# Gate and up projections of a quantised FFN from bare 4-bit values, with the PSUM bank rescaled between scale groups

## What is computed

```python
vals = _FP4_LUT[nib].reshape(out_f, in_p * 8)      # 0, 0.5, 1 ... 6 and their negatives
w = vals * repeat(scales.T, 128, axis=1)           # gate_up: [2*1408, 512], 4 groups of inputs
gate_up = x @ w_gu.T;  h = silu(gate) * up         # I = 1408
y = h @ w_down.T;  y / sqrt(mean(y * y) + 1e-6)    # down: 11 groups of inputs
```

## Time and profile before

| | us |
|---|---|
| median of 3 runs | 812.85 (810.42 to 815.97) |
| the profiled execution | 812.29 |
| its span, first to last instruction | 810.5 |
| PE busy in the span | 716.4 (88%) |
| DVE busy | 498.3 (61%) |
| ACT busy | 386.4 (48%) |
| POOL busy | 195.8 (24%) |

### The profile page before, as it was taken

The page is one execution under the profiler, slowest core; times in us unless marked ns, Lnnn a source line. Parts: engine busy times, 40 slices in busy tenths (PEclk is TensorE's granted clock), DMA queues, the critical chain, the costliest instruction groups (busy, mean ns, idle before and its releaser), DMA issues.

```text
span 810.5 us, 11696 instructions
## 1 busy us (share of the span) xinstructions
PE 716.4 (88%) x4565; PEld 571.0 (70%) x4574; DVE 498.3 (61%) x956; ACT 386.4 (48%) x617; POOL 195.8 (24%) x229
## 2 busy tenths in 40 slices
PE   5899999999999996689998898898988898899993
PEld 4688777887777785467676666676667676678883
DVE  4658668765587667667456567665577575643424
ACT  4345453447444633743635363646463745452324
POOL 0554344454453559411210000211000211000000
PEclk9999999999999998679999999999999999999997
DMA  9500101003200310120001130030120030000201
GB/s 324 181 16 10 44 2 40 15 1 118 66 14 2 118 54 1 66 90 1 1 27 52 53 104 0 1 130 0 53 105 0 1 130 0 20 34 1 104 1 53
DMA packets 25408, 41.17 MB, mean 51 GB/s; under 512 B 5002, under 2 KB 7690, under 8 KB 25226
## 3 DMA queue, kind: packets, MB, share of 16 engines
q1 hardware_dynamic: 23194, 37.40, 13.4%
q10 hardware_dynamic: 2160, 3.02, 1.1%
HBM read 28.88 MB, written 11.53 MB: 50 GB/s over the span
## 4 chain that ended last, share of the span: by engine, by line
PE 57%; DVE 22%; ACT 14%; issue 3%; POOL 1%; DMA 1%; ACTq 1%; SPq 0%; DVEq 0%; POOLq 0%
PE ps L1716 14%; PE ps L1730 11%; PE ps L1304 10%; PE ps L1388 3%; PE ps L1693 3%; PE ps L529 2%; PE ps L1694 2%; PE ps L1343 2%; PE ps L538 2%; DVE small L417 2%; ACT w L280 2%; DVE act_s L378 2%; DVE w L410 2%; DVE masked L1223 2%; DVE act_s L410 1%
## 5 line engine op out<-in xcount | busy, mean ns | idle before, releaser
L1716 PE MATMUL ps<-x2T_hi,weights 128*128 128x512 f32 x528 | 164.1, 392 | 0.0
L1716 PEld LDWEIGHTS ps<-x2T_hi,weights 128*128 128x128 f32 x528 | 99.9, 189 | 20.4
L1730 PE MATMUL ps<-weights,h_hi 128*128 128x512 f32 x352 | 110.8, 397 | 0.7 <-DVE h_lo L1578 0.6
L1716 PE MATMUL ps<-x2T_lo,weights 128*128 128x512 f32 x264 | 108.6, 411 | 0.4
L1601 DVE TENSOR_TENSOR silu<-ps,silu 128x512 f32<-128x512 f32 x44 | 30.4, 690 | 124.0 <-PE ps L1716 106.3
L1304 PE MATMUL ps<-wqkv_lo,xT_hi 128*128 128x512 f32 x192 | 81.3, 424 | 9.7 <-DVE wqkv_lo L1172 5.7
L1730 PEld LDWEIGHTS ps<-weights,h_hi 128*128 128x128 f32 x352 | 66.9, 191 | 16.0 <-DVE h_lo L1578 1.8
L1304 PE MATMUL ps<-wqkv_hi,xT_hi 128*128 128x512 f32 x192 | 76.6, 399 | 0.0
L1304 PE MATMUL ps<-wqkv_hi,xT_lo 128*128 128x512 f32 x192 | 76.4, 398 | 0.0
L1100 POOL TENSOR_TENSOR rot<-qkv,tab 128x256 f32<-128x256 f32 x64 | 44.8, 733 | 116.1 <-ACT qkv L989 116.1
L1730 PE MATMUL ps<-weights,h_lo 128*128 128x512 f32 x176 | 69.4, 394 | 0.0
(11 more groups left out here) (190 smaller groups left out, 1518.9 us busy)
## 6 DMA issues: line engine op xcount, KB each, us to landing
w<-in_fside_BxS2xS_dram SPq DMA_DIRECT2D x4, 1024.0 KB, 5.3
x_dram<-xb SPq DMA_DIRECT2D x4, 1024.0 KB, 4.3
xc<-x_dram SPq DMA_DIRECT2D x4, 1024.0 KB, 5.6
x_in<-in_x_dram SPq DMA_DIRECT2D x15, 256.0 KB, 3.5
xb<-x_dram SPq DMA_DIRECT2D x3, 1024.0 KB, 5.6
out_dram<-xc SPq DMA_DIRECT2D x3, 1024.0 KB, 4.3
z<-in_x_dram SPq DMA_DIRECT2D x3, 768.0 KB, 5.0
x_dram<-z SPq DMA_DIRECT2D x3, 768.0 KB, 3.5
```

Of the source, the lines that this page charges most:

```text
L1716: last = nc.tensor.matmul(dst[:, :], lhs, rhs, start=False, stop=(k == NK - 1 and n == 2), skip_group_check=True)
L1730: last = nc.tensor.matmul(ps[c][:, :], lhs, rhs, start=(it == 0 and n == 0), stop=(it == NI - 1 and n == 2))
```

## The change

Gate and up keep bare values in all four groups. A group is two matmuls (values by `x2T_lo`, values by `x2T_hi`) per half, and after groups 0, 1 and 2 the bank is multiplied in place by the ratio of this group's scale to the next one's; the last scale goes into the silu's `scale` and into the product with up. Gate is now rescaled by ACT (`scale_gate`), up by DVE (`scale_up`), three times each per tile. The ratios are made once on DVE (`column_ratios`, after chunk 1; a zero scale becomes 2^-80).

What comes with it:

- A tile is cut into four rounds. A round is group k of gate, group k of up and one chunk (three matmuls) of a down product; there are now 44 places per batch, one behind each round (place n is behind round n mod 4 of tile n div 4).
- All 24 gate and up pieces are bare. ACT copies the ones of even number, DVE those of odd number; only the 11 down pieces still take a diagonal, `hi` and `lo`. 18 pieces are made in chunks 14 and 15 and behind them, 17 beside the first batch (`PIECE_SLOTS`). The last layer norm of attention (`LATE_STEPS`) moves into the first batch as well.
- The output of down is copied out of its banks at the start of the next batch (`copy_y`, DVE, four times), and the residual and final scaling of the output (before on DVE) are done by POOL. So are the column scaling of the expert's weights (through a copy of the row on ACT, `w_rows_out`, `v_rows_out`) and the sum behind the expert (`add01`, `add23`).
- `EXPERT_STEPS`, `EXPERT0_STEPS` and `OUTPUT_STEPS` have new places; two maxima of the batch after next are taken at places 40 and 43.

```diff
+EXPERT_STEPS = {"w_maxima": 0, "w_maxima2": 4, "x_maxima": 2, "columns": 6, "x_maxima2": 5, "ratio": 6, "root": 7,
+                "smooth": 7, "rows": 8, "scale_x": 8, "max_x": 8, "round_x": 10, "clip_x": 11, "w_rows_out": 10,
+                "pool_scale_w": 11, "max_w": 13, "xq01": 13, "w_scale": 15, "round_w": 14, "clip_w": 16, "xq23": 13,
+                "wq01": 17, "wq23": 18, "products01": 19, "rescale01": 19, "products23": 21, "rescale23": 21,
+                "silu": 21, "gate": 23, "v_maxima": 22, "a_maxima": 23, "ratio2": 24, "columns2": 24, "root2": 25,
+                "smooth2": 26, "rows2": 27, "v_rows_out": 28, "pool_scale_v": 25, "scale_a": 28, "max_v": 29,
+                "round_v": 30, "clip_v": 30, "v_scale": 30, "max_a": 30, "round_a": 33, "clip_a": 33, "vq": 34,
...
+AHEAD_STEPS = {"w_maxima": 43, "w_maxima2": 40}
+OUTPUT_STEPS = {"rms": 1, "inverse": 2, "residual": 7, "moments": 18, "root": 20, "inverse2": 33, "output": 34}
+ROUNDS = 4
...
+FIRST_BESIDE = 18
+PIECES_AT = {(14, "masks"): (0,), (14, "split"): (1, 2, 3, 4), (14, "end"): (5, 6), (15, "masks"): (7, 8, 9, 10),
+    (15, "split"): (11, 12, 13, 14), (15, "end"): (15, 16, 17)}
...
+PIECE_SLOTS = (1, 2, 9, 16, 20, 21, 23, 25, 25, 26, 26, 28, 29, 31, 32, 33, 36)
...
+LATE_STEPS = {"z_moments": 0, "z_root": 7, "z_shift": 9, "z_x1": 12}
...
+                nc.gpsimd.tensor_tensor(src[:, c, 0:width], src[:, c, 0:width], self.rows[:, 0:width], ALU.mult)\
+                    .then_inc(self.columns_scaled, 1)
...
+        elif self.copied_by[m] == "dve":
+            dve.wait_ge(full, at + 1)
+            self.nc.vector.tensor_scalar(self.parts(m)[0], bank[:, 0:self.count(m) * P], 1.0, None, ALU.mult)\
+                .then_inc(drained, 1)
...
+            nc.vector.reciprocal(later, scales[:, GU_TILES:SCALES[0]]).then_inc(ratio_step, 1)
+            dve.wait_ge(ratio_step, 3)
+            before = slice(0, SCALES[0] - GU_TILES)
+            nc.vector.tensor_tensor(ratios[:, before], scales[:, before], later, ALU.mult).then_inc(ratio_step, 1)
...
-        def scale_up(b, it):
-            act.wait_ge(up_unscaled, b * NI + it + 1)
-            nc.scalar.activation(ps[5][:, :], ps[5][:, :], ACT.Copy, scale=weights.unscaled_scale(1, it))\
-                .then_inc(up_scaled, 1)
+        def scale_gate(b, it, k):
+            act.wait_ge(gate_part, (b * NI + it) * (NK - 1) + k + 1)
+            nc.scalar.activation(ps[4][:, :], ps[4][:, :], ACT.Copy, scale=weights.column(k, 0, it))\
+                .then_inc(gate_scaled, 1)
...
+            if it + 1 < NI:
+                scale_gate(b, it + 1, 0)
             hidden_hi(b, it)
-            if it + 1 < NI:
-                scale_up(b, it + 1)
...
-            beside(3 * it + 1)
-            beside(3 * it + 2)
+            beside(ROUNDS * it)
+            for k in range(1, NK - 1):
+                if it + 1 < NI:
+                    scale_gate(b, it + 1, k)
+                beside(ROUNDS * it + k)
...
+            for c in range(NC):
+                nc.gpsimd.tensor_scalar(y_sum[:, c, :], y_sum[:, c, :], f_small[:, 2, c:c + 1], None, ALU.mult)\
+                    .then_inc(y_scaled, 1)
+            for c in range(NC):
+                pool.wait_ge(y_scaled, b * NC + c + 1)
+                nc.gpsimd.tensor_tensor(xc[:, c, :], xc[:, c, :], y_sum[:, c, :], ALU.add).then_inc(f_z, 1)
...
-        def scale_gate(b, it):
-            dve.wait_ge(gate_unscaled, b * NI + it + 1)
-            nc.vector.tensor_scalar(ps[4][:, :], ps[4][:, :], weights.unscaled_scale(0, it), None, ALU.mult)\
-                .then_inc(gate_scaled, 1)
+        def scale_up(b, it, k):
+            dve.wait_ge(up_part, (b * NI + it) * (NK - 1) + k + 1)
+            nc.vector.tensor_scalar(ps[5][:, :], ps[5][:, :], weights.column(k, 1, it), None, ALU.mult)\
+                .then_inc(up_scaled, 1)
...
+            nc.vector.tensor_scalar(y_sum[:, c, :], ps[c][:, :], 1.0, None, ALU.mult).then_inc(y_copied, 1)
...
-                for n, (lhs, rhs) in enumerate(passes((*weights.gate_up(k, half, it), x2T_hi[:, k, :],
-                                                       x2T_lo[:, k, :]))):
-                    last = nc.tensor.matmul(dst[:, :], lhs, rhs, start=False, stop=(k == NK - 1 and n == 2),
-                                            skip_group_check=True)
-            return last
...
+            if k > 0:
+                pe.wait_ge(scaled, (b * NI + it) * (NK - 1) + k)
+            elif it > 0:
+                pe.wait_ge(h_done if half else silu_done, b * NI + it)
+            values = weights.gate_up(k, half, it)
+            nc.tensor.matmul(dst[:, :], values, x2T_lo[:, k, :], start=(k == 0), stop=False, skip_group_check=True)
+            nc.tensor.matmul(dst[:, :], values, x2T_hi[:, k, :], start=False, stop=True, skip_group_check=True)\
+                .then_inc(part if k < NK - 1 else whole, 1)
...
-            hidden(b, it, 0, ps[4]).then_inc(gate_ps, 1)
-            beside(3 * it)
-            hidden(b, it, 1, ps[5]).then_inc(up_ps, 1)
-            beside(3 * it + 1)
-            if it + 1 < NI:
-                unscaled_gate(b, it + 1)
-            if it == 0:
-                unscaled_up(b, it + 1)
-            else:
-                if it == 1:
-                    pe.wait_ge(f_z, b * NC + 1)
-                down(b, it - 1, next_unscaled)
-            beside(3 * it + 2)
+            if it > 0:
+                down(b, it - 1, 2)
+            if it == NI - 1:
+                down(b, it - 1, 3)
+                for k in range(NK):
+                    beside(ROUNDS * it + k)
+                return
+            groups(b, it + 1, 0)
+            if it > 0:
+                down(b, it - 1, 3)
+            beside(ROUNDS * it)
+            groups(b, it + 1, 1)
+            down(b, it, 0)
+            beside(ROUNDS * it + 1)
+            groups(b, it + 1, 2)
+            down(b, it, 1)
+            beside(ROUNDS * it + 2)
+            groups(b, it + 1, 3)
```

More of the change, by code:

```diff
@@ L154, in weight_pieces @@
-    gate_up(0)
-    for pair in range(1, PAIRS - 2):
+        pieces.append(("down", it, 0, 0, 6 * NK * E + 2 * E * it))
+    for pair in range(PAIRS - 2):
         gate_up(pair)
-        down(2 * pair - 2)
-        down(2 * pair - 1)
-    for it in range(2 * PAIRS - 6, 2 * PAIRS - 4):
+    for it in range(7):
         down(it)
     gate_up(PAIRS - 2)
+    down(7)
+    down(8)
     gate_up(PAIRS - 1)
-    for it in range(2 * PAIRS - 4, NI):
-        down(it)
-    return pieces, at
+    down(9)
@@ L212, with quantised_before @@
     _turns[expert_bank(_use)] += 1
+def quantised_before(layer, weights):
+    return 2 + (not weights) if layer else weights
 class Expert:
@@ L704, in diagonals @@
     def diagonals(self, pool, m):
-        kind, where, k, tiles, _ = PIECES[m]
+        it = PIECES[m][1]
         before = [n for n in SCALED if n < m and DIAG_OF[n] == DIAG_OF[m]]
@@ L1720, in down @@
[L1720 to L1736 removed]
+                weights.wait_ready(pe, PIECE_OF["gate_up", it // 2, k])
@@ new lines, in groups, with down @@
+        def groups(b, it, k):
+            group(b, it, k, 0)
+            group(b, it, k, 1)
+        def down(b, it, c):
+            if c == 0:
+                pe.wait_ge(h_lo_done, b * NI + it + 1)
+                if b == 0:
+                    weights.wait_ready(pe, PIECE_OF["down", it, 0])
+            if it == 0:
+                if b == 0:
+                    pe.wait_ge(weights.attention_drained[c], ATTENTION_TURNS[c])
+                else:
+                    pe.wait_ge(y_copied, (b - 1) * NC + c + 1)
+            cols = slice(c * P, (c + 1) * P)
+            for n, (lhs, rhs) in enumerate(passes((h_hi[:, it % 2, cols], h_lo[:, it % 2, cols], *weights.down(it)))):
+                last = nc.tensor.matmul(ps[c][:, :], lhs, rhs, start=(it == 0 and n == 0),
+                                        stop=(it == NI - 1 and n == 2))
+            if it == NI - 1:
+                last.then_inc(y_ps, 1)
+            elif c == NC - 1:
+                last.then_inc(down_read, 1)
```

448 lines of the change are left out of this document (216 added, 232 removed), and 3 rows, old and new, of the table EXPERT_STEPS.

## The result

| | us |
|---|---|
| the changed kernel, median of 4 runs | 828.36 (826.8 to 833.83; a fifth run took 824.39) |
| the kernel before, beside it, median of 4 runs | 813.24 (810.42 to 815.97) |
| ratio of the two | 1.0186, 95% interval 1.0127 to 1.0245 |
| the profiled execution of the changed kernel | 833.83, span 831.8 |

The change makes the kernel slower by 1.9% (1.3 to 2.4). The forecast was 802, its range 764 to 826. In a second measurement the ratio was 1.0155 [1.0119, 1.0191]. The profiled execution is the slowest of the four, 5.5 us above their median.

The account below looks back on a forecast made before the run. PE was taken to set the pace in the FFN batches, with no engine full just ahead of them. From 812.3 us, -19 (transition), +11.9 (batch 0), +2.6 (middle batches) and -5.5 (last) gave 802.3, forecast 802, range 764 to 826.

Parts of the forecast that it names:

- What leaves PE: FFN tiles: 28 matmuls of 512 columns instead of 34, 60.2 us less on PE, 15 per batch.
- The mechanism of a middle batch: FFN batches 1 and 2: PE's 15 us return as waits for DVE and ACT; 121.1 us, +1.3 each.
- The blocks behind `h_lo`: DVE's scaling and maxima of the expert's activations in FFN batches delay PE by 5.0 and 2.4 us a batch.
- Nothing waits for them until 20 or more rounds later: Weight scaling (2.49 us a batch) and output residual and scaling (some 4.7), moved to POOL, count as nothing on PE.
- the tail is the same code: The stretch behind the last matmul stays unchanged, at 12.3 us.
- Batch 0: First FFN batch, with 50 us of foreign work including moved pieces and attention's last normalisation: 130.7 us, +11.9.
- Batch 3: Last FFN batch, no expert beside it, the only one keeping a third of PE's saving: 87.4 us, -5.5.
- The bank: Between attention and FFN: pieces issued inside chunks 14 and 15, first transpose near 328 instead of 347, -19 us.
- POOL beside DVE: FFN batches: POOL's work slows a quarter of 11 `h_lo` on DVE, 2 us a batch; 8 if all were caught.
- A: Rival, chance 0.27: FFN waits hide in each other; 766 us if half the new waits vanish, 738 if all.
- B: Rival, chance 0.18: PE's long waits in batches with an expert also lower its clock, up to 43 us, 845.

Follow-up runs that it names:

- the kernel before with two passes: Kernel before the change, with one of three matmuls of groups 1 to 3 left out and nothing else changed: 788.85 us, 0.968.
- the idle matmuls: On the early output, PE issues matmuls of zeros ahead of its long waits and ahead of the transposes of batches 1 to 3: 811.24 us, 0.998.
- the early output: Changed kernel with POOL's normalised output at place 24 instead of 34, its reciprocal at 22 instead of 33: 821.83 us, 1.0088.
- the residual on DVE: On top of the idle matmuls, the output's residual back from POOL to DVE, one fused instruction at each of four places: 808.19 us, 0.9936.
- the first expert's maxima as before: On top of the residual on DVE, the first expert's three column maxima at the chunks they had before the change: 809.1 us, 0.9917.

## Why the prediction was wrong, step by step

- **What leaves PE**: right. 264 matmuls, 60.2 us, and 66 per batch in the counts.
- **The mechanism of a middle batch**: right in kind. "PE's 15 us return as waits for DVE and ACT" is what the profile shows, and the kernel before with two passes shows it without any rescaling: 3.6 of 15 us are kept. Which waits, I had wrong: not mostly the rescaling of up (4.4 us of batch 1), but the silu and the product with up once a tile (10.1). The size was off: 126.5 and not 121.1. Three parts of it were measured. *The clock*: I gave it no term, only a rival with 0.18, since batch 1 of before kept 0.99 with 13.2 us of idle PE. The changed kernel's waits are longer (3.62 and 3.43 us in batch 1 and 4.8 at its start, where the longest before were 2.2 within the tiles and 1.6 at the start), and the idle matmuls put the clock's price at 4.1 us a batch, as much as three quarters of the 5.4 missing. By the Trainium skill, "TensorE: Matmul & The Clock Gate", section "A second HAM failure mode: psum-queue depth-cycling", idle times between groups of matmuls cost clock; the trace agrees (0.93, and 1.00 once they are filled). The loss is not in every round, though: in batch 1 it stands in the stretch to the first silu, the third and the fifth tile, beside a few long waits. *POOL*: 3.5 to 3.7 us where I had 2, of which the late `h_lo` that I meant is 0.8. *The blocks behind `h_lo`*: 1.4 to 2.2 where I had 7.4, an error to the other side. Together they come to about nothing (4.1 and 1.6 us up, 5.2 to 6.0 down), so the 5.4 us are not wholly traced to terms of the sum, and that it came near 121 at all is partly luck: errors that cancel.
- **"Nothing waits for them until 20 or more rounds later"** and **"the tail is the same code"**: wrong, and this step was mine to see. POOL's output is waited for by SP's store, and behind the store stand two loads. The late load of w cost 4.6 us at the head of batch 2, 2.6 in the batch as a whole, and the late load of xc 3.6 in the tail; the early output gave back 6.1 by the medians.
- **Batch 0**, 130.7: measured 134.0 and then 129.0; right within its scatter.
- **Batch 3**, 87.4: measured 89.0. The undisturbed tile takes 6.8 us, not 6.4 + 0.2, from silu to silu; without rescalings it takes 6.6, and with the same number of matmuls in the kernel before 6.3 to 6.4.
- **The bank**, -19: the first transposes came at 337.9 and 335.6, not 328. Behind attention's last matmul 3.7 us of pieces remained that I had left out; the rest is attention itself, which ended at 327.9 to 334.1 in 12 profiles of the changed kernel and its variants (331.0 in the mean), at 328.3 and 327.7 in two of the kernel before. It goes with the granted clock from 50 to 150 us, as told above; why the clock is lower there in most runs is open, and the column maxima are not shown to be the cause.
- **POOL beside DVE**: the mechanism was right, its share in the loss was not. "SBUF — State Buffer", section "Who interferes with whom", in the Trainium skill says that a DVE instruction with two SBUF inputs contends with a GpSimd instruction that reads SBUF; `h_lo` has its 1460 ns with POOL's steps and never over 694 ns without them. But at most one `h_lo` of 11 in a middle batch was caught so fully, not a quarter of them.
- **The rivals.** A needed the waits to hide in each other; PE's idle time of 24.8 us denies it. B was the case to weigh more: I priced it at up to 43 us in three batches, and it took about 4 in each of the middle ones. With the late loads (6), the pieces left out (3.7) and attention's 3 that was enough to pass 821.

Of the changed kernel's profiled 833.8 against the forecast's 802.3, 31.5 us, the stages give 9.9, 3.3, 5.4, 7.8, 1.6 and 3.3, 31.3 together. Some 5 of them are that execution's own, which is 5.5 us above the median.

The kernel with the early output, idle matmuls and the residual on DVE is 2.2% faster than the changed kernel (0.9936 to 1.0155, each against the kernel before) and 0.6% [0.4, 0.9] faster than the kernel before. Of the versions that compute the whole only the one with the first expert's maxima as before (0.9917) measured lower, and the two intervals meet.
